# A four-block graph residual network: an earlier adjacency cast, matmuls ahead of the data, another order on VectorE, and ScalarE's normed rows in block 3

## The reference

```python
x = _layernorm(x + _L0_gnn_ref(x, adj, W_stack))   # two attention layers
x = _layernorm(x + _L1_gnn_ref(x, adj, W))         # normalised sums over neighbours
x = _layernorm(x + _L2_gnn_ref(x, adj, ...))       # mean of neighbours, self term
x = _layernorm(x + _L3_gnn_ref(x, adj, ...))       # two sums with a relu between
```

```python
Wh, Ws = split(x @ W, 2)
a = softmax(Wh @ Ws.T) * adj
x = leaky_relu(a @ Wh + x, 0.01)
```

## Time and profile before

| | us |
|---|---|
| median of 3 runs (lowest, highest) | 749.22 (748.46, 749.93) |
| the profiled execution | 749.87 |
| its span, first to last instruction | 748.1 |
| TensorE busy in it | 720.9 |
| VectorE busy | 481.1 |
| ScalarE busy | 337.9 |
| GpSimd busy | 321.7 |

### The profile page before, as it was taken

One profiled execution on the slowest core, in us unless ns is written; L12 is line 12 of the kernel. 1 busy time (PEld: TensorE's weight loads), 2 busy tenths in 40 slices (PEclk: granted clock), 3 DMA queues, 4 the chain that ended last, 5 costly groups with the idle time before them and its releaser, 6 DMA issues.

```text
span 748.1 us, 13194 instructions
## 1 busy us (share of the span) xinstructions
PE 720.9 (96%) x3962; PEld 612.2 (82%) x3962; DVE 481.1 (64%) x1110; ACT 337.9 (45%) x785; POOL 321.7 (43%) x345
## 2 busy tenths in 40 slices
PE   6997999999999999999999999989999999999996
PEld 5886888888888888888888888878877787689985
DVE  3764777777777656465665665763677757875466
ACT  3754556656555565455565465451222412221112
POOL 0143676767676514645536445474665000003200
PEclk9998999999999999999999999999999999999999
DMA  7014233242423031433123232245762221210012
GB/s 266 29 57 169 85 124 130 94 158 84 162 92 112 29 127 57 103 120 130 71 88 122 70 99 112 71 101 126 185 182 90 71 63 57 71 43 3 1 43 73
DMA packets 63139, 72.39 MB, mean 97 GB/s; under 512 B 36336, under 2 KB 56432, under 8 KB 58992
## 3 DMA queue, kind: packets, MB, share of 16 engines
q1 hardware_dynamic: 63088, 71.78, 30.2%
HBM read 46.60 MB, written 16.78 MB: 85 GB/s over the span
## 4 chain that ended last, share of the span: by engine, by line
PE 87%; DVE 5%; issue 3%; ACT 2%; DMA 2%; POOL 1%; SPq 0%; DVEq 0%; POOLq 0%; ACTq 0%
PE scores L1891 37%; PE ob L1891 27%; PE tb L1891 9%; PE tb L2043 7%; PE xb L1891 3%; DMA keep<-in_x 1%; DMA arow<-in_adj 1%; PE tb L1987 1%; DVE zb L1668 1%; DVE norm_values L1674 1%; ACT prob L872 1%; PE xb L2068 1%; PE tb L1910 0%; DVE zb L1601 0%; PE xb L1933 0%
## 5 line engine op out<-in xcount | busy, mean ns | idle before, releaser
L668 POOL TENSOR_TENSOR prob<-prob,arow 128x512 f32<-128x512 f32 x128 | 189.9, 1506 | 151.4 <-ACT prob L872 151.3
L1891 PE MATMUL ob<-val,stationary 128*128 128x512 f32 x960 | 188.1, 346 | 0.0
L1891 PEld LDWEIGHTS ob<-val,stationary 128*128 128x128 f32 x960 | 147.9, 190 | 18.6
L1219 DVE TENSOR_TENSOR stationary<-tb,stationary 128x512 fp32r<-128x512 f32 x128 | 85.4, 687 | 59.7 <-ACT stationary L773 58.5
L1891 PE MATMUL scores<-wst_h,whs_h 128*128 128x512 f32 x256 | 102.7, 401 | 0.0
L1891 PE MATMUL scores<-wst_h,whs_l 128*128 128x512 f32 x256 | 100.0, 391 | 0.0
L1891 PE MATMUL scores<-wst_l,whs_h 128*128 128x512 f32 x256 | 99.8, 390 | 0.0
L1309 DVE TENSOR_REDUCE row_values<-scores 128x1 f32<-128x512 f32 x128 | 85.7, 682 | 13.2 <-PE scores L1891 11.9
L773 ACT ACTIVATE stationary<-tb 128x512 fp32r<-128x512 f32 x128 | 72.8, 594 | 45.3 <-PE tb L2043 43.8
L872 ACT ACTIVATE prob<-scores,row_values 128x512 f32<-128x512 f32 x128 | 86.7, 689 | 11.4 <-DVE row_values L1316 11.4
L2043 PE MATMUL tb<-ident,prob 128*128 128x128 f32 x512 | 72.7, 274 | 0.3 <-DVE stationary L1219 0.3
(11 more groups left out here) (224 smaller groups left out, 1202.0 us busy)
## 6 DMA issues: line engine op xcount, KB each, us to landing
arow<-in_adj SPq DMA_DIRECT2D x32, 1024.0 KB, 5.1
adjacency_halves<-arow SPq DMA_DIRECT2D x16, 512.0 KB, 3.0
features_scratch<-xs SPq DMA_DIRECT2D x32, 128.0 KB, 1.9
xres<-features_scratch SPq DMA_DIRECT2D x32, 128.0 KB, 2.2
keep<-in_x SPq DMA_DIRECT2D x4, 512.0 KB, 7.1
xres<-in_x SPq DMA_DIRECT2D x16, 128.0 KB, 2.0
self_term_scratch<-rst SPq DMA_DIRECT2D x16, 128.0 KB, 1.7
rin<-self_term_scratch SPq DMA_DIRECT2D x16, 128.0 KB, 2.2
```

The costliest lines, as they stand in the source:

```text
L668: nc.gpsimd.tensor_tensor(prob[u][:, cs], prob[u][:, cs], arow[u][:, cs], ALU.mult).then_inc(g.msk.sem, 1)
L1219: return nc.vector.tensor_tensor(dst, v, h.bitcast(F32), ALU.subtract)
L1891: return nc.tensor.matmul(o, l, r, start=start, stop=stop)
```

## The change

- Start: GpSimd rounds the first half of layer 0's weight columns and ScalarE only the second; VectorE makes the low parts of the first half between those of the two feature halves. TensorE runs eight 128 x 128 matmuls of the identity before the first chunk and three after it. It turns chunk 1 only after the two query parts of chunk 0's projection, and the first part takes each half of the features as it comes.
- Attention, layer 0: the cast of tile 1's adjacency goes from behind tile 1's exponentials to ahead of them, behind tile 0's first two chunks.
- End of the attention: TensorE makes the first two sums of the last tile each one step earlier, and VectorE makes `n_moving` of tile 12 two steps earlier.
- Blocks 1 and 2: in VectorE's slot `residual` goes ahead of `rows_lo`.
- Block 3: VectorE makes only a shift (minus the mean times the reciprocal, 128 x 1), and ScalarE makes the normed rows with it.

```diff
@@ gpsimd
+            pool.wait_ge(s_wgraw[0], 16)
+            nc.gpsimd.tensor_copy(wg_h[:, :, 0:D], wg_raw[:, :, 0:D]).then_inc(s_wqh, 1)
             pool.wait_ge(s_bias, 32)
@@ scalar
-            copy(wg_h[:, :, :], wg_raw).then_inc(s_wgh[0], 1)
+            copy(wg_h[:, :, D:2 * D], wg_raw[:, :, D:2 * D]).then_inc(s_wgh[0], 1)
             features(1)
...
                         hi(*p, 1)
+                    if first:
+                        cast_halves(b, u)
                     if fin:
                         rows_hi(*before(b, u, 2))
...
                         n_moving(b + u - 4, u)
-                    if first:
-                        cast_halves(b, u)
...
+            def normed(t):
...
+                act.wait_ge(s_shift, t + 1)
...
+                ge(act, F.out[t % 4], 16 * (t // 4))
+                nc.scalar.activation(finished[t % 4][:, :], zb[u][:, :], ACT.Identity, bias=nmax[u][:, :],
+                                     scale=rstd[:, u:u + 1]).then_inc(F.new.sem, 1)
...
                                 sums_hi(LEAD.index(t))
+                            if t:
+                                normed(t - 1)
                             deviation(t // 2 * 2, t % 2)
+                        normed(NT - 1)
@@ vector
-            features(0)
+            feature(0, 0)
+            dve.wait_ge(s_wqh, 1)
+            rest(wg_l[:, :, 0:D], wg_raw[:, :, 0:D], wg_h[:, :, 0:D]).then_inc(s_wgl[0], 1)
+            feature(0, 1)
             dve.wait_ge(s_wgh[0], 1)
-            rest(wg_l[:, :, :], wg_raw, wg_h[:, :, :]).then_inc(s_wgl[0], 1)
+            rest(wg_l[:, :, D:2 * D], wg_raw[:, :, D:2 * D], wg_h[:, :, D:2 * D]).then_inc(s_wgl[0], 1)
             features(1)
...
             finish5(NT - 2, 0)
+            n_moving(NT - 4, 0)
             n_lo(NT - 3, 1)
             row_sum(NT - 2, 1)
-            n_moving(NT - 4, 0)
...
-                        ge(dve, a.out[t % 4], 16 * (t // 4))
-                        nc.vector.tensor_scalar(finished[t % 4][:, :], zb[u][:, :], mv[:, u, 0:1], rstd[:, u:u + 1],
-                                                ALU.subtract, ALU.mult).then_inc(a.new.sem, 1)
+                        ge(dve, a.new, t - 1)
+                        nc.vector.scalar_tensor_tensor(nmax[u][:, :], mv[:, u, 0:1], -1.0, rstd[:, u:u + 1],
+                                                       ALU.mult, ALU.mult).then_inc(s_shift, 1)
...
                         if ep:
                             total(*p)
+                        if ep:
+                            residual(*p)
                         if fin:
                             rows_lo(*pp)
                         if ep:
-                            residual(*p)
                             norm(*p)
@@ tensor
+            keep_busy(8)
             features(0)
-            features(1)
+            keep_busy(3)
...
-                pe.wait_ge(s_wgl[l], 1)
-                if l:
-                    ge(pe, G[l - 1].ex, 4 * NT)
-
                 pe.sem_inc(g.prod.sem, 1)
...
+                pe.wait_ge(s_wgl[l], 1)
+                if l:
+                    ge(pe, G[l - 1].ex, 4 * NT)
...
+                    if not l and isinstance(i, int) and i + o == 0:
+
+                        for k in range(KT):
+                            pe.wait_ge(s_x0l, k + 1)
+                            mm(bank[:, :], wg_h[:, k, os], xtall_h[:, k, gs], k == 0, False)
+                            mm(bank[:, :], wg_h[:, k, os], xtall_l[:, k, gs], False, False)
+                            last = mm(bank[:, :], wg_l[:, k, os], xtall_h[:, k, gs], False, k == KT - 1)
...
-                        if not l and o == KT and i in (1, 2):
+                        if not l and o == KT:
                             features(i + 1)
+                            if i == 0:
+                                pe.wait_ge(s_wgl[0], 2)
...
+            attend(NT - 2, 1, 0)
             turn(NT - 2, 1, 2)
             n_rows(NT - 4, 0)
-            attend(NT - 2, 1, 0)
+            attend(NT - 2, 1, 1)
             turn(NT - 2, 1, 3)
-            attend(NT - 2, 1, 1)
```

More of the change, by code:

```diff
@@ L240, in adjacency_resnet @@
         s_wgh = [sem(f"gat_weight_hi_{l}") for l in range(LAYERS)]
+        s_wqh = sem("gat_query_weight_hi")
         s_wgl = [sem(f"gat_weight_lo_{l}") for l in range(LAYERS)]
@@ L376, in adjacency_resnet @@
         s_fl = sem("block3_sums_lo")
+        s_shift = sem("block3_shift_ready")
         s_kb = sem("block3_residual_biased")
@@ L1092, in sums_hi @@
                 copy(fsum_h[:, first * P:stop * P], fbank[q][:, 0:(stop - first) * P]).then_inc(s_fh, 1)
+            def normed(t):
+                u = t % 2
+                act.wait_ge(s_shift, t + 1)
+                if t < 2:
+                    ge(act, C.out[u], 8 * NT)
+                    ge(act, C.xtr, NT)
+                elif t < 4:
+                    ge(act, Dg.y, NT)
+                ge(act, F.out[t % 4], 16 * (t // 4))
+                nc.scalar.activation(finished[t % 4][:, :], zb[u][:, :], ACT.Identity, bias=nmax[u][:, :],
+                                     scale=rstd[:, u:u + 1]).then_inc(F.new.sem, 1)
             def general():
@@ L1219, in rest, with feature @@
                 return nc.vector.tensor_tensor(dst, v, h.bitcast(F32), ALU.subtract)
+            def feature(i, k):
+                dve.wait_ge(s_x0h, KT * i + k + 1)
+                gs = slice(i * CH, (i + 1) * CH)
+                rest(xtall_l[:, k, gs], tb[k][:, :], xtall_h[:, k, gs]).then_inc(s_x0l, 1)
             def features(i):
                 for k in range(KT):
-                    dve.wait_ge(s_x0h, KT * i + k + 1)
-                    gs = slice(i * CH, (i + 1) * CH)
-                    rest(xtall_l[:, k, gs], tb[k][:, :], xtall_h[:, k, gs]).then_inc(s_x0l, 1)
+                    feature(i, k)
             def weights():
@@ L1905, in features @@
                     if i == 1:
-                        pe.wait_ge(s_x0l, k + 1)
+                        pe.wait_ge(s_x0l, KT)
                     elif i:
@@ L1924, in weights, with keep_busy @@
                     last.then_inc(s_w2t, 1)
+            def keep_busy(n):
+                for _ in range(n):
+                    mm(xb0[:, 0:P], ident[:, :], ident[:, :], True, True)
+            keep_busy(8)
             features(0)
-            features(1)
+            keep_busy(3)
             def n_rows(t, u):
@@ L1964, in project_part @@
                     gs, os = bass.ts(i, CH), slice(o * P, (o + 1) * P)
+                    if not l and isinstance(i, int) and i + o == 0:
[4 more added lines that the diff above has]
+                            last = mm(bank[:, :], wg_l[:, k, os], xtall_h[:, k, gs], False, k == KT - 1)
+                        last.then_inc(g.prod.sem, 1)
+                        return
                     exact3(bank[:, :], [(wg_h[:, k, os], wg_l[:, k, os], xtall_h[:, k, gs], xtall_l[:, k, gs])
@@ L1968, in project @@
                 def project(i):
-                    rows_turned(i)
+                    if l or i:
+                        rows_turned(i)
                     for o in range(2 * KT):
-                        if not l and o == KT and i in (1, 2):
+                        if not l and o == KT:
                             features(i + 1)
+                            if i == 0:
+                                pe.wait_ge(s_wgl[0], 2)
                         if o < KT:
```

## The result

The changed kernel takes 751.23 us (median of 10 runs, 750.96 to 751.58) and the one before, on the same chip, 749.12. The ratio is 1.0024 with a 95% interval of 1.0014 to 1.0033: slower by 2.1 us, where 744.6 was predicted. The profiled execution has a span of 749.4, against 748.1 in the profiled one of before.

What follows compares the result with a forecast made beforehand. TensorE, 87% of the chain, was taken as the bound; -7.6 - 2.8 - 0.6 + 6.0 + 0.4 = -4.6 us gave a median of 744.6 us, range 738.5 to 750.1.

Steps and rivals of the forecast that it cites:

- the second cast: Attention layer 0: moving the cast up makes tile 2's slot an ordinary one, 13.09 instead of 20.73 us: -7.6 us.
- the start: First projection: identity matmuls, earlier low weights and later chunk 1 transposes end it at 15.0 instead of 17.82: -2.8 us.
- end of the attention: Last tile's first sums go into TensorE's 1.32 us wait there: -0.6 us, bounds 0 and -1.3.
- VectorE's order in blocks 1 and 2: Residual, statistics and mean ahead of the low half lengthen a loop that crowded projections pay: +6.0 us.
- block 3: Normed rows on ScalarE take about 0.50 us and the shift adds a step: +0.4 us, mostly at the last tile.
- the turn: Blocks 1 and 2: loop round the engines between low halves, 5.11 and 4.07 us, paid by six crowded projections in each.
- The stall of the first two projections: Block 1: a low half queued behind tile 2's residual, which awaits its DMA, delays the projection: +1.8 us.
- a slot above 5.3 everywhere: Sign of a wrong forecast: slots longer than TensorE's own 5.3 us of work per tile in block 1.
- VectorE's slot becomes the bound of both blocks: Rival: residual held up by GpSimd lengthens the loop: 754.3 us, chance 0.1; block 1 alone 750.1, chance 0.1.
- so the tail keeps its pace: Block 3's tail: ScalarE's rows and VectorE's two-tile wait leave the pace unchanged, within the +0.4 us term.
- The new order costs nothing: Rival: VectorE's new order in blocks 1 and 2 is free, giving 738.6 us; chance 0.2.
- Tables: Rival: in block 3 Identity and square root need separate tables, two loads per tile, some 770 us; chance 0.02.

Runs made afterwards that it cites:

- run 7: The kernel before with only the second cast (tile 1's adjacency) moved up: 741.22 us, ratio 0.9891.
- run 8: The kernel before with the changed start alone (identity matmuls, GpSimd's cast of half the weights, chunk 1's turns later): 746.61 us, ratio 0.9968.
- run 3: The changed kernel with the old order in blocks 1 and 2 and block 3's normed rows back on VectorE: 738.64 us, ratio 0.9859.
- run 1: The changed kernel with rows_lo ahead of residual again in blocks 1 and 2: 740.76 us, ratio 0.9883.
- run 4: The kernel before with only the new order of residual and rows_lo: 758.9 us, ratio 1.0127.
- run 2: The changed kernel with block 3's normed rows on VectorE again and no shift: 748.82 us, ratio 0.999.
- run 6: The changed kernel with the old order in block 1 and the new one in block 2: 743.59 us, ratio 0.9923.
- run 5: The changed kernel with the low half put between residual and statistics, in blocks 1 and 2: 741.59 us, ratio 0.9896.
- run 11: As run 1 (block 3's rows on ScalarE), with a third buffer for block 3's sums: 739.26 us, ratio 0.9866.
- run 10: As run 3, without the eleven identity matmuls of the start: 740.19 us, ratio 0.988.

## Why the prediction was wrong, point by point

| term | predicted | by the trace of after | on the chip |
|---|---|---|---|
| the second cast | -7.6 | -7.65 (slot) | -7.9 (run 7) |
| the start | -2.8 | -2.9 (values turned) | -2.55 (run 8) |
| end of the attention | -0.6 | -0.6 | not run alone (+0.2 left by runs 3, 7 and 8) |
| VectorE's order in blocks 1 and 2 | +6.0 | +10.3 | +10.5 (run 1), +9.95 (run 4) |
| block 3 | +0.4 | +2.1 | +2.4 (run 2), +2.1 (runs 1, 3) |
| sum | -4.6 | +1.3 (spans) | +2.1 (medians) |

**The second cast and the start** were right in place and size. TensorE was next in line in tile 2's slot, as said. **The end of the attention** was right in place, for the wait of the earlier trace rows is gone; its size is not shown. It is read from the lead alone: 11.2 at block 1, less 7.65 and 2.9. On the chip run 3 gains 10.3 where runs 7 and 8 together gain 10.5, which leaves +0.2 for it, with an interval of more than 1 us either way.

**VectorE's order in blocks 1 and 2** is the step that failed, and by the size of a term, for the mechanism was the one described: runs 1, 4 and 6 put the loss there, run 5 shows that the turn's length is what is paid. I added the turn up to 5.11 in block 1 and 4.07 in block 2; it is 5.34 and 4.32. Two pieces were too short. Projection to self term is 2.25 (542.87 to 545.12), not 2.15: I took it from a projection of the earlier trace rows that met no crowd, where the first matmul takes 0.39 instead of 0.50. And additions to residual are 1.04 (545.51 to 546.55), not 0.91: that was the distance to a low half in the earlier trace rows, which doesn't use the additions' result and starts before the second of them has ended (549.64 and 0.48), while the residual does use it and starts 0.04 behind its end (546.03 and 0.48). A quarter of a microsecond looks small, but it is paid in each of twelve crowded turns: 1.4 us in block 1 and 1.4 in block 2, beside the +3.4 and +0.8 predicted. The rest, about 1.7, I did not price at all: the tiles after the crowded ones (+0.9 in block 1, +0.4 in block 2) and the step from block 1 to 2 (+0.35), where I let TensorE's own work hide the turn. The stall of the first two projections came to 1.55 for my 1.8, by the lead at the second. Had I added the turn up to 5.34, it would have been over the 5.3 of TensorE's own work, and my sign of being wrong, a slot above 5.3 everywhere, came true in block 1 for all but one distance: from the second projection to the fifteenth they are 5.34 to 5.65, and 5.28 once.

The rival "VectorE's slot becomes the bound of both blocks" came nearest with its 750.1 and 754.3, and in its outcome it came true for block 1, but that was luck: it was tied to a residual held up by GpSimd, and that condition did not come. In the new order the residual starts 0.14 ahead of GpSimd's sum, as my argument against this rival had it, and takes 0.42. I had priced the turn once, at its lowest, and hung the upper end on a separate event; so the range ended at 750.1, below the measured time.

**Block 3** failed at "so the tail keeps its pace". The wait was named there (VectorE's addition waits for the rows of two tiles before), and not added up: from the start of the addition to the reciprocal 0.34, to the statistics 0.12, to the shift 0.34, to ScalarE's rows 0.18, their 0.60 and 0.13 to the addition make 1.71 where VectorE alone had 1.33. The rows' 0.60 was taken as 0.50, from a row with one pointer operand. The Trainium skill (ScalarE: Activation LUTs, section What ACT_TABLE_LOAD costs) gives 186 ns and 0.833 ns per element for an activation and about 93 ns for each pointer operand; with two of them that estimates 0.585 for 256 columns, and the trace agrees with it. The last tiles lost 1.4 us behind the last matmul (4.32 to 5.73), the other part went in the matmuls before it, where the last group's rounded sums queue behind rows and a square root on ScalarE: TensorE waits 1.25 us for them, and 0.47 in the kernel before.

**The other rivals.** *The new order costs nothing* fell at once with the spacing. *Tables*: no load stands at the rows' line, and the sixteen loads are those of before.

## What to carry to other kernels

When an edit moves work of one engine ahead of something that another engine waits for, follow the wait all the way round: if it comes back to the same engine, the sum of the turn is paid at every tile, so each piece has to come from a row with the same dependence, and the sum's own error has to go into the range, times the number of turns. Moving a step off a busy engine was no gain here, where its result comes back to that engine through a buffer of two tiles, nor with one of three (run 11). And the smallest move is worth trying between the two orders: residual ahead, statistics and mean behind the low half cost some 0.8 us (runs 5 and 1) where the whole block ahead cost 10.5.

## What the runs showed of the hardware that was not expected

**Who pays for a collision.** In run 3, with the old order, GpSimd's sum starts 0.08 us ahead of VectorE's residual:

```profile
538.73 0.73 POOL L752 TENSOR_TENSOR rin<-pm 128x256 f32<-128x256 f32 x1 [1.63 <-DVE zb L1628]
538.81 0.94 DVE L1692 SCALAR_TENSOR_TENSOR zb<-zb,xres 128x256 f32<-128x256 f32 x1
```

The residual takes 0.94 and the sum 0.73. In the changed kernel the residual starts 0.14 ahead (546.55 and 546.69 above), and it takes 0.42 and the sum 0.89. Block 1's groups by line agree (duration in ns: least, median, most), of run 3 and then of the changed kernel, the residual first:

```profile
L1692 DVE SCALAR_TENSOR_TENSOR zb<-zb,xres x14: 415/803/946, 519.9 to 584.0; 128x256 f32<-128x256 f32 x14
...
L752 POOL TENSOR_TENSOR rin<-pm x12: 731/738/744, 518.0 to 571.9; 128x256 f32<-128x256 f32 x12
```

```profile
L1695 DVE SCALAR_TENSOR_TENSOR zb<-zb,xres x14: 416/425/991, 519.3 to 591.7; 128x256 f32<-128x256 f32 x14
...
L752 POOL TENSOR_TENSOR rin<-pm x12: 741/885/892, 519.3 to 579.4; 128x256 f32<-128x256 f32 x12
```

The instruction that starts second is the longer one, whichever engine it is on. It need not be GpSimd's sum: in run 3 a residual that starts at 534.63, 0.01 behind GpSimd's next cast, takes 0.88. The Trainium skill (GPSIMD Engine Reference, section Specifications) says that the two contend when VectorE's instruction has two SBUF inputs; the rows agree with that.

**The pace at the start.** In run 10 the granted clock reads 1.00 from 4.5 us on, while six matmuls of 512 columns come 0.43 us apart and the later ones 0.23. The second is the pace of the earlier trace rows (0.231) and the first nearly half of it, as if the clock stood at the lower of its two levels; that it did, no row shows. Ahead of the slow ones TensorE had made eight turns and waited 1.16 us; ahead of the first projection in the changed kernel it had been at identity matmuls and turns since 1.54. In the long slot of the kernel before, the granted clock did show the lower level (0.50); here the pace has to be read from the starts of the matmuls.
